# Start of the attention in a fused transformer block: the first maxima turned earlier, one batch's queries and statistics later

## The reference

```
x = x + tanh(g_xattn) * attention(layernorm(x), ctx, ctx)      # 32 query heads, 8 key heads, head size 16
x = x + tanh(g_ffn) * ffn(layernorm(x))
# attention: weights = softmax(q k / 4); out = weights v, per batch, 128 queries by 128 keys
# ffn: h_bitlinear(silu(h_bitlinear(h, w_gate)) * h_bitlinear(h, w_up), w_down)
# h_bitlinear(x, w): x through a Hadamard transform and 8-bit rounding by its largest value,
#                    w rounded to -1, 0, 1 times its mean size, then the matmul
```

## Time and profile before

| | |
|---|---|
| median of the runs | 466.92 us |
| the profiled execution's own time | 466.68 us |
| its span, first to last instruction | 464.8 us |
| PE, DVE, ACT, POOL busy | 97%, 82%, 63%, 46% |
| granted TensorE clock, mean | 1.00 |

### The profile page before, as it was taken

One profiled execution on the slowest core, in us unless ns is written; L12 is line 12 of the kernel. 1 busy time (PEld: TensorE's weight loads), 2 busy tenths in 40 slices (PEclk: granted clock), 3 DMA queues, 4 the chain that ended last, 5 costly groups with the idle time before them and its releaser, 6 DMA issues.

```text
span 464.8 us, 9025 instructions
## 1 busy us (share of the span) xinstructions
PE 450.1 (97%) x3112; PEld 285.9 (61%) x3112; DVE 382.1 (82%) x703; ACT 293.5 (63%) x522; POOL 214.6 (46%) x331
## 2 busy tenths in 40 slices
PE   8999999999999989989999999999999999999997
PEld 7655555554555434469844578954469964479664
DVE  5889998787968749859998967998976999888892
ACT  3498987677768779877747327643616753657460
POOL 4355556988997544755007634203926200920000
PEclk9999999999999999999999999999999999999999
DMA  8999120022023050001100650100460110242077
GB/s 249 328 349 350 35 52 18 17 59 25 13 42 103 17 188 5 1 1 25 24 0 6 117 149 11 23 12 0 83 158 31 24 25 0 41 90 53 1 146 216
DMA packets 68183, 35.90 MB, mean 77 GB/s; under 512 B 50288, under 2 KB 62960, under 8 KB 68144
## 3 DMA queue, kind: packets, MB, share of 16 engines
q1 hardware_dynamic: 67408, 34.48, 28.9%
q10 hardware_dynamic: 736, 0.92, 0.6%
HBM read 19.26 MB, written 4.19 MB: 50 GB/s over the span
## 4 chain that ended last, share of the span: by engine, by line
PE 74%; POOL 8%; issue 6%; DVE 6%; ACT 4%; DMA 1%; POOLq 0%; DVEq 0%; ACTq 0%
PE ps L886 16%; PE ps L963 12%; PE ps L940 11%; PE ps L615 7%; PE ps L637 5%; PE ps L680 5%; PE ps L952 3%; PE ps L954 3%; PE ps L697 3%; PE ps L829 2%; PE ps L645 2%; PE ps L822 1%; PE ps L739 1%; DVE wst L1491 1%; DVE wst L1486 1%
## 5 line engine op out<-in xcount | busy, mean ns | idle before, releaser
L886 PE MATMUL ps<-wst 128*128 128x512 bf16 x512 | 113.1, 379 | 2.3 <-DVE wst L1486 2.0
L1317 DVE TENSOR_REDUCE reg<-ps 128x4 f32<-128x512 f32 x128 | 81.7, 683 | 22.9 <-PE ps L637 21.3
L886 PEld LDWEIGHTS ps<-wst 128*128 128x128 bf16 x512 | 49.2, 98 | 62.3 <-DVE wst L1486 4.0
L579 POOL TENSOR_TENSOR reg_rest<-reg_rest,z_sc 128x1024 f32<-128x1024 f32 x24 | 47.4, 2010 | 82.7 <-DVE z_sc L1528 82.7
L1044 ACT ACTIVATE reg<-ps 128x512 f32<-128x512 f32 x116 | 62.9, 597 | 25.1 <-PE ps L645 24.8
L637 PE MATMUL ps<-reg 32*128 32x256 f32 x512 | 72.6, 400 | 0.3 <-ACT reg L1071 0.2
L1180 ACT ACTIVATE wst<-wst 128x512 f32<-128x512 f32 x64 | 40.1, 628 | 51.6 <-DVE wst L1486 51.2
L615 PE MATMUL ps<-reg 32*128 32x512 f32 x232 | 70.1, 639 | 0.0
L940 PE MATMUL ps<-had_f,wst 128*128 128x128 f32 x512 | 67.1, 276 | 1.1 <-DVE wst L1491 1.1
L940 PEld LDWEIGHTS ps<-had_f,wst 128*128 128x128 f32 x512 | 64.0, 191 | 4.4 <-DVE wst L1491 1.8
L1210 ACT CAST y_split<-ps 128x512 fp32r<-128x512 f32 x64 | 37.4, 586 | 34.0 <-PE ps L940 34.0
(11 more groups left out here) (171 smaller groups left out, 747.6 us busy)
## 6 DMA issues: line engine op xcount, KB each, us to landing
wst<-in_w SPq DMA_DIRECT2D x16, 512.0 KB, 8.4
reg<-in_w SPq DMA_DIRECT2D x8, 512.0 KB, 5.1
out<-x_all SPq DMA_DIRECT2D x16, 256.0 KB, 2.1
x_all<-in_x SPq DMA_DIRECT2D x3, 1024.0 KB, 8.8
reg<-in_v SPq DMA_DIRECT2D x4, 256.0 KB, 4.4
reg<-in_k_t SPq DMA_DIRECT2D x28, 32.0 KB, 2.6
x_all<-in_x ACTq DMA_DIRECT2D x1, 512.0 KB, 4.3
reg_rest<-reg SPq DMA_TRANSPOSE x20, 3.0
```

The lines of the kernel that those rows point to most:

```text
L579: pool.tensor_tensor(z, z, sc, ALU.mult).then_inc(sem("z_scaled"), 1)
L886: last = pe.matmul(ps[:, banks[ob % n], :], tern_gu[:, ob // 2, m, j, P * (ob % 2):P * (ob % 2) + P], q1_t[:, j, :], start=(j == 0), stop= ...
L1317: dve.tensor_reduce(neg_max[n % 2][:, g:g + 2, i + m, :], ps[:, row_bank(r, m), :].rearrange("p (g a t) -> p g a t", g=2, a=2), AX_X, ALU. ...
```

## The change

PE turns the maxima of batch 0 right after quarter (-1, 3), where it had turned the queries of batch 2. These follow as the second piece of `step(0)`, behind `quarter(0, 0)`. The bank that both write changes its waits accordingly: the turning of the maxima waits for the second copy of queries, that of batch 2's queries for the copy of the maxima, that of batch 3's queries for the third copy of queries. Of the two spins and four spins at this place two stay. ACT copies the maxima ahead of the queries of batch 2, with `normalise_q(3)` still behind both. DVE takes `maximum(1, 2)` (the seventh) before `statistics_q(3)` (the fourth).

```diff
@@ turn_max(n)
                 else:
-                    pe.wait_ge(sem("qt_done"), 3)
+                    pe.wait_ge(sem("qt_done"), 2)
@@ turn_queries(n)
-                if n == 3:
+                if n == 2:
                     pe.wait_ge(sem("mt_done"), 1)
-                elif n == 1:
+                elif n == 1 or n == 3:
                     pe.wait_ge(sem("qt_done"), n)
-                elif n == 2:
-                    pe.wait_ge(sem("qt_done"), 2)
@@ step(b) on PE
                 quarter(b, 0)
+                if b == 0:
+                    turn_queries(2)
                 weigh(b - 1, 1)
@@ PE, before the loop
             quarter(-1, 3)
-            turn_queries(2)
+            turn_max(0)
             spin(2)
-            turn_max(0)
-            spin(4)
             for b in range(NB - 2):
@@ ACT, before the loop
             normalise_q(2)
+            copy_max(0)
             copy_queries(2)
-            copy_max(0)
             normalise_q(3)
@@ DVE, before the loop
             maximum(1, 1)
+            maximum(1, 2)
             statistics_q(3)
-            maximum(1, 2)
```

## The result

The changed kernel took 470.27 us (median of 12 executions, 467.15 to 477.43), the kernel before 466.75 (12, 466.25 to 470.59). The ratio is 1.0056, with a 95% interval of 1.0033 to 1.0080; executions far above the rest (474.7 and more, here three) are left out of ratios. The forecast of 467.6 had the direction and not the size, and the median lies above its range.

The account below looks back on a forecast made before the run. The first exp sets the pace in step 0, PE after step 1 begins. PE's 1.9 us gain counts 0, +0.9 and -0.1 give +0.8 us, so 467.6 us; range 466.2 to 469.3.

Parts of the forecast that it names:

- Part 1: PE turns the maxima earlier, with fewer spins ahead of quarter(0, 0), which starts at 18.1, 1.9 us earlier.
- Part 2: Batch 2's queries behind quarter(0, 0): ACT's copy ends at 21.2; the two and four spins that went only filled time.
- Part 3: Later statistics on DVE, or the queries' copy, delay normalise_q(3) on ACT; first exp at 22.3 instead of 21.39, +0.9 us.
- Part 4: From the first exp on, step 0 is the same round trip shifted, 0.08 us given back: step 1 starts +0.8 us.
- the sum: Whole kernel: PE's hidden 1.9 us counts 0, then +0.9 and -0.1, together +0.8 us; forecast 467.6.
- that rival: Later exps in step 0 catch up and absorb the delay; time stays at 466.9; chance 0.14.
- The rival with the clock: PE's quiet stretch from 20.6 to 22.95 lowers the clock: 1.7 us lost (469.3) or 4.3 (471.9); chance 0.08.
- The rival in which the gain comes through: First exp runs at 19.5, once its columns are there; 1.9 us gained, 465.0; chance 0.08.

Follow-up runs that it names:

- the swap alone: Kernel before with only DVE's order changed, seventh maxima ahead of the fourth statistics: 467.31 us, ratio 1.0005.
- the kernel with the statistics back: Changed kernel with DVE's order as before, fourth statistics ahead of the seventh maxima: 471.17 us, ratio 1.0115.
- four spins as filler: Changed kernel with four spins put behind the third batch's queries in step 0: 467.46 us, ratio 1.0021.
- the filler's trace: Profiled execution of the changed kernel with eight spins put behind the third batch's queries in step 0: 467.83 us, ratio 1.0028.
- the first exp at 19.56: Changed kernel with ACT's first two exps ahead of the copy of the third batch's queries and the normalising: 465.67 us, ratio 0.9966.
- its spins put back ahead: Changed kernel with the four removed spins put back ahead of quarter(0, 0), nothing behind the queries: 470.08 us, ratio 1.0057.

## Why the prediction was wrong

- **Part 1 and 2 (PE's order).** Right. From the rows of batch 1 on (16.26 before, 16.74 here), `quarter(0, 0)` came 1.95 us later in the changed kernel and 3.75 before: 1.8 us gained of a forecast 1.9, and in that kernel none of it reached the end. (Of the six spins four went, as Part 1 counts them, and not all, as Part 2 says.)
- **Part 3 (the exp behind the normalising).** Right. Forecast +0.9 for the first exp; +0.86 in the changed kernel net of its late landing, and 22.28 for the swap alone. That both paths hold is shown by the kernel with the statistics back.
- **Part 4 and the sum.** Right at full clock: +0.8 forecast; 0.6 in the one execution of the changed kernel, 0.8 with four spins as filler, 0.7 for the swap alone. Nothing was absorbed in steps 0 and 1, so that rival falls.
- **The rival with the clock.** This is the step that failed: the sum has no term for the clock, and the rival that has one got a chance of 0.08 with the reason "2.3 us is short, and full work follows". The runs show the opposite. That stretch of 2.3 us was followed by a fall in 11 of 12 executions, and a stretch as long, made in the kernel before by nothing but three copies on ACT, in 4 of 4. No row weighed for or against it: the idle time of 1.36 us at 170.40, at full clock, was there to be read, but it has full work right ahead of it and so is 1.4 us of quiet and not 2.3. The rival had the place, the consequence and the size of one short fall: 1.7 us forecast, 1.2 in the trace, 1.5 to 2.6 between the three executions of 0.996 and the one of 1.000 (the 2.6 has the late landing in it). It took the length of a fall from the start of the kernel, 3.6 us of matmuls of 421 ns. The profile's own granted clock reads 1.00 there, but 421 ns is what the same matmul takes under 0.50 in the filler's trace. The fall of the profiled execution lasts 3.41 us. In eight of the 11 the mean clock says that it was longer, so that the median lies at 470.27 and not at 469.3. The range ended where the short fall did.
- **No gain.** The rival in which the gain comes through did not happen, but its condition names what to do: the first exp must not stand behind the normalising. With the first exp at 19.56, where that rival wanted it, 0.9 us are gained, and not its 1.9, since the second exps still start only at 22.54, with the queries' copy and the normalising ahead of them on ACT.

What stays open: what sets how long a fall lasts (means of 0.996 to 0.982 in one kernel), what causes the falls that begin ahead of the change (from 16.4 and 16.9 us in two traces), and where those of the kernel before begin.

## What to carry to other kernels

An engine that arrives earlier at work which waits for another engine gains nothing; look first at what stands directly ahead of the released instruction in the other engine's list, here a normalising that no exp needed. When an edit makes PE wait longer at one place, weigh that wait by what the clock may do, and not only by its length: in this kernel 0.6 us more of waiting cost 3.8 us. Count with it what PE does just ahead: an idle time of 1.36 us with full work on either side cost no clock. Filler matmuls help in the wait itself; the same number a few microseconds ahead of it did not.

## What the runs showed of the hardware

A quiet stretch of PE of 2.2 to 2.3 us (one column product on one of the four strips, then 1.26 to 1.54 us of idle time) went with a fall of the mean granted clock in 24 of 27 executions of four kernels. One execution of each was profiled, and there the granted clock is 0.50 for 3.4 to 6.8 us, from a moment between 0.1 us before the end of the wait and 1.7 us after it. Where the same product stood with 0.39 to 0.90 us of idle time (1.4 to 1.6 us of quiet), falls came in 3 of 35 executions of three kernels, no more than in the kernel before with its 8 of 79. Idle times of 1.36 us right behind full work had the granted clock at 1.00 after them in 13 of 13 traces. The Trainium skill's page "TensorE: Matmul & The Clock Gate" (Part 1) says that the throttled state is the default and that activity releases it. The traces agree, with 1.22 us for 0.70 in two records of the same product in the fallen stretch, and with the clock back at 1.00 at 28.68 while PE is busy without a break; in the kernel with its spins put back ahead it is back only at 31.4, after 6.8 us of such work.
